# Reordering the last twelve tiles of the prologue of an attention and feed-forward kernel: four tiles of v last, a flag one tile sooner, statistics in one place

## Time and profile before

| | us |
|---|---|
| median of 3 runs | 3751.72 (3751.03 to 3753.09) |
| the profiled execution's own time | 3749.25 |
| its span | 3747.5 |
| TensorE busy | 3704.4 (99%) |
| VectorE, ScalarE, GpSimd busy | 3153.3, 2795.3, 622.9 |

### The profile page before, as it was taken

How to read it: one execution, slowest core, us unless ns; L and a number is a source line. 1 busy time by engine, 2 the same in 40 slices (tenths; PEclk the granted TensorE clock), 3 DMA queues, 4 the chain that set the end, 5 groups by cost and what they waited for, 6 DMA issues and landing times.

```text
span 3747.5 us, 57714 instructions
## 1 busy us (share of the span) xinstructions
PE 3704.4 (99%) x21736; PEld 2051.2 (55%) x21736; DVE 3153.3 (84%) x2918; ACT 2795.3 (75%) x3626; POOL 622.9 (17%) x281
## 2 busy tenths in 40 slices
PE   7999999999999999999999999999999999999999
PEld 6344444444444444444444444444468888888887
DVE  6899999999999999999999999988875555555554
ACT  4788888888888888888888888889873333333333
POOL 0101001023434343223222301320020000000000
PEclk9999999999999999999999999999999999999999
DMA  7544444445444544554555444544340101010010
GB/s 246 125 104 101 105 105 105 106 99 110 101 101 101 111 106 96 112 113 104 113 110 117 98 99 103 120 100 115 78 152 23 45 23 45 23 45 23 29 40 23
DMA packets 255351, 344.58 MB, mean 92 GB/s; under 512 B 118000, under 2 KB 142576, under 8 KB 254000
## 3 DMA queue, kind: packets, MB, share of 16 engines
q1 hardware_dynamic: 251504, 324.43, 36.8%
q0 software_dynamic: 3392, 15.73, 1.4%
q10 hardware_dynamic: 128, 0.03, 0.0%
HBM read 198.55 MB, written 131.07 MB: 88 GB/s over the span
## 4 chain that ended last, share of the span: by engine, by line
PE 89%; DVE 7%; issue 2%; ACT 1%; DMA 0%; DVEq 0%; ACTq 0%; SPq 0%
PE ps L887 22%; PE ps L862 16%; PE ps L956 13%; PE ps L1014 12%; PE ps L800 9%; DVE acc L1652 5%; PE ps L942 5%; PE ps L803 4%; PE ps L910 3%; PE ps L961 2%; PE ps L772 1%; PE ps L1050 1%; ACT pr L1282 1%; PE ps L923 1%; PE ps L1035 1%
## 5 line engine op out<-in xcount | busy, mean ns | idle before, releaser
L1282 ACT ACTIVATE pr<-ps 128x1024 f32<-128x1024 f32 x2048 | 1990.4, 1029 | 257.6 <-PE ps L862 251.0
L1652 DVE TENSOR_TENSOR acc<-acc,pr 128x2048 f32<-128x2048 f32 x768 | 1780.7, 2319 | 41.1 <-ACT pr L1282 11.7
L887 PE MATMUL ps<-pr,vst 128*32 128x512 f32 x8192 | 1011.2, 600 | 0.0
L862 PE MATMUL ps<-qst,kst 50*128 50x512 f32 x4096 | 781.9, 456 | 9.9 <-ACT pr L1282 7.5
L862 PEld LDWEIGHTS ps<-qst,kst 50*128 50x128 f32 x4096 | 337.2, 184 | 658.8 <-ACT pr L1282 463.7
L887 PEld LDWEIGHTS ps<-pr,vst 128*32 128x32 f32 x8192 | 213.3, 109 | 446.6 <-issue 433.5
L1451 ACT ACTIVATE rb<-ps,scf 128x512 f32<-128x512 f32 x228 | 157.0, 689 | 350.5 <-PE ps L961 350.5
L1014 PE MATMUL ps<-tP,hh_ 128*128 128x512 f32 x1024 | 399.6, 390 | 1.4 <-DVE hl_ L1873 1.4
L1014 PE MATMUL ps<-tP,hl_ 128*128 128x512 f32 x1024 | 398.8, 389 | 0.0
L800 PE MATMUL ps<-xt,wqh 128*128 128x512 f32 x1024 | 376.8, 419 | 3.0 <-DVE xt L1542 3.0
L478 POOL TENSOR_SCALAR xin<-xin,mv,rs 128x512 f32<-128x512 f32 x60 | 205.7, 3432 | 876.5 <-DVE rs L1571 876.5
(11 more groups left out here) (179 smaller groups left out, 3822.8 us busy)
## 6 DMA issues: line engine op xcount, KB each, us to landing
qst<-q_scratch SPq DMA_DIRECT2D x128, 256.0 KB, 4.7
kst<-k_scratch SPq DMA_DIRECT2D x128, 256.0 KB, 7.1
q_scratch<-stg SPq DMA_DIRECT2D x112, 256.0 KB
k_scratch<-stg SPq DMA_DIRECT2D x112, 256.0 KB
qst<-q_scratch SPq DMA_DIRECT2D x128, 128.0 KB, 5.0
kst<-k_scratch SPq DMA_DIRECT2D x128, 128.0 KB, 7.8
vst<-v_scratch SPq DMA_DIRECT2D x128, 128.0 KB, 4.7
xr<-in_L_attn_x_dram SPq DMA_DIRECT2D x64, 256.0 KB
```

The costliest lines, as they stand in the source:

```text
L862: ins = e.matmul(ps[:, 2 * c + hh, :], kst[rows, r, j, t * 128:(t + 1) * 128], qst[rows, r, j, c * 512:(c + 1) * 512], start=True, stop=True)
L887: ins = e.matmul(ps[32 * c4:32 * c4 + 32, 4 + j, :], vst[:, r, t, 32 * hh:32 * hh + 32], pr[:, sl, c, hh, :], start=(t == 0), stop=(t == 7 ...
L1282: e.activation(pr[:, sl, c, :, :], ps[:, 2 * c:2 * c + 2, :], ACT.Exp, scale=SCALE).then_inc(s_exp, 1)
L1652: e.tensor_tensor(acc[:, j, :], old, new, ALU.add).then_inc(s_add, 1)
```

## The change

The second chunk's order becomes the eight tiles of q and k and then the four of v: T = 12 to 19 are Q8 to Q15, T = 20 to 23 are V4 to V7. Everything of the flag moves one T: TensorE's part and ScalarE's transfers from 21 to 20, VectorE's first part from 20 to 19 and its second from 21 to 20, where it stands behind the last turn of the third chunk. The third chunk's statistics and gathering all run at T = 14 and its refining and normalizing at T = 15; before they ran at T = 14 (three statistics), 15 (the fourth, gathering) and 16 (refining, normalizing). The first and second chunk's statistics stay where they were.

```diff
-         (0, 1, 8, 2, 3, 4, 5, 6, 7, 9, 10, 11))
+         (0, 1, 2, 3, 4, 5, 6, 7, 8, 9, 10, 11))
...
-                if T == 21:
+                if T == 20:
                     pe_tile(e, T, T % 4, 0, 10)
                     pe_flag(e, 0)
                     pe_tile(e, T, T % 4, 10, 12)
...
-                if T == 21:
+                if T == 20:
 
                     sync_shift(e, 0)
...
-                for n in ((0, 1, 2), (3, 4), range(6, 11))[k + 3] if -3 <= k < 0 else ():
+                steps = ((range(5), range(6, 11), ()) if C else ((0, 1, 2), (3, 4), range(6, 11)))
+                for n in steps[k + 3] if -3 <= k < 0 else ():
                     dve_ln_step(e, C + 1, n)
                 if T - 1 in UNIT_AT:
                     dve_ternary(e, UNIT_AT.index(T - 1))
-                if T == 20:
+                if T == 19:
                     dve_flag(e, 0, 0)
                 if 0 <= k < 4:
                     dve_turn(e, C + 1, k, 4 + k)
-                if T == 21:
+                if T == 20:
                     dve_flag(e, 0, 1)
                     flag = load_flag(e, 0)
                     dve_shift(e, flag, 0)
```

## The result

The changed kernel takes 3759.64 us (median of 13 runs, 3754.28 to 3763.01), the kernel before in the same series 3751.31 (13 runs, 3748.08 to 3754.71): 8.3 us more, ratio 1.0021, 95% interval 1.0014 to 1.0028. The forecast was 3759.2. The profiled execution took 3759.76, with a span of 3758.0 against 3747.5 before, so the two traces stand 10.5 apart where the medians stand 8.3 apart; the profiled execution of before was one of its faster ones, by 2 us.

What follows compares the result with a forecast made beforehand. TensorE, busy 99% of the span, bounds the kernel. First score +7.9 and clock -0.4 sum to +7.5: profiled 3749.25 becomes 3756.8, against the median 3759.2 us; range 3753.2 to 3761.5.

Steps and rivals of the forecast that it cites:

- V6's copy waits for V4's store: ScalarE before the first score: V6's copy waits for V4's store to land at 105.7, first score 108.7, +7.9.
- SyncE reaches V4 at 95.2: SyncE's queue: V4's store, behind Q10 to Q15, is issued at 96.53 - 1.28 = 95.2; bound below 93.9.
- Landing 10.5 after the issue, by V5's row: V4's store takes V5's 10.5 from issue to landing, behind Q15: 95.2 + 10.5 = 105.7.
- The low bound from V0's 5.4: Earliest landing of V4's store, with V0's time, little ahead of it: 93.9 + 5.4 = 99.3.
- V6 to V7, 2.89: ScalarE behind V6's copy: `woh` and V7's copy take 2.89 more, and the first score waits for V7.
- The clock, -0.4: TensorE after the longer stall: first scores slow (+0.3), up to 1.3 could come back before the first sum; middle -0.4.
- The turn sooner by 1.85, the flag sooner: Prologue: third chunk's first turn 1.85 sooner, flag one tile sooner; these alone would bring the first score 2.6 sooner.
- The first load of q: SyncE's first q and k loads: issued about 1.3 later, landing near 94.3, covered by the first score at 108.7.
- After the first score nothing follows that depends on the clock of the prologue: First pair: the first score's gain or loss carries to the end in full; sums run at VectorE's own pace.
- rival (b): V4's store: no backlog reaches it, issued by 89, so the flag chain decides: -2.6, 3749.1; chance 0.05.
- The Trainium skill's ring order: Transfer engines: descriptors go in ring order, done only when all engines are, so V4 cannot pass Q15's backlog.
- The Trainium skill's fit of 2.0 us plus size over 436 GB/s: V4's store: 2.6 us estimated for 256 KB, landing 97.8, first score 100.8, no loss; no v store was that short.

Runs made afterwards that it cites:

- 1: Changed kernel with V6 staged in an area of its own, so its copy waits for no store: 3749.89 against 3750.29 for the kernel before.
- 3: Changed kernel with the third chunk's statistics back where they were, only order and flag changed: 3757.50 against 3750.29 for the kernel before.
- 5: Changed kernel with V4's store ahead of Q14's and Q15's in SyncE's queue: 3753.27 against 3750.62 for the kernel before.
- 2: Kernel before with only the third chunk's statistics and normalizing moved as in the change: 3750.04 against 3750.29 for the kernel before.
- 7: Kernel 1 with the staging slots of Q8 to Q15 in the order of their stores: 3750.74 against 3750.62 for the kernel before.
- 9: Kernel 7 with VectorE's second part of the flag ahead of the last turn's low part: 3751.03 against 3750.62 for the kernel before.
- 6: Changed kernel with rounded parts of Q14 and Q15 stored twice, ahead of V4's store: 3763.01 (5 runs) against 3750.03 for the kernel before.
- 4: Changed kernel with V4's store issued by ScalarE on its own queue: 3753.05 against 3750.29 for the kernel before.
- 8: Kernel before with the third chunk's statistics moved and staging slots reordered, measured twice: 3748.83 against 3750.62, then 3751.63 against 3750.03.

## Why the prediction was right

It was right in direction, size and mechanism; some terms were off, and one assumption fell. That the number came within 0.5 us is luck. In the traces the first score is 10.3 later and the span 10.5 longer, where I had 7.9 and 7.5: SyncE's queue and the clock together were some 3 us worse than forecast. The medians lie only 8.3 apart, because the execution of before that I counted from was 2 us faster than its median and the changed kernel's stands at its own.

- **V6's copy waits for V4's store: right.** Taking that wait away takes the loss away (1).
- **SyncE reaches V4 at 95.2: too early, 97.64.** The later start of VectorE has no part in it: at 70.7 the two queues stood at the same place. I had everything to Q15 come sooner by V4's 1.28. Without V4 the queue took from 70.72 to 97.6, 26.9 us, where with V4 it had taken 25.8; in 3 it took 26.5. Taking a v store out of the queue did not shorten it in these traces. Why was not tested, and the queue's pace differs by execution: from Q10's to the end of Q13's store it took 20.5 in the changed kernel and 17.2 in 5, with the same transfers.
- **Landing 10.5 after the issue, by V5's row: right**, 10.4 in the changed kernel, 10.5 in 3. The low bound from V0's 5.4 did not come near: 8.7, with two stores fewer ahead and a queue that had stood still for 4 us (5), is the shortest seen.
- **V6 to V7, 2.89: right**, 108.12 to 111.00.
- **The clock, -0.4: wrong sign.** From the first score to the first sum it took 7.4 (118.53) instead of 7.1. The four slow matmuls cost their 0.5 and nothing came back: the granted clock was still 0.50 from 112 to 116 and 0.56 from 116 to 120.
- **The turn sooner by 1.85, the flag sooner:** 1.45 against the shifted start, and `mh` was issued at 93.33 where I had 91.6: 0.97 is the shift, 0.40 the turn, 0.44 the slow matmuls behind it. The first load of q was issued 3.7 later (81.66 against 77.93), not 1.3. All were hidden behind V6's wait, as forecast, and what was won there had no worth (3).
- **"After the first score nothing follows that depends on the clock of the prologue": wrong.** It holds for a loss. For a gain the exponentials meet stores that have not landed, and VectorE and TensorE meet x and v (1, 2, 7, 9). So the rival (b), -2.6, would by 1 have been nearer 0 even with its landing. The step that I left out is `act_exp`'s wait on the stores whose slots it overwrites: I had named no work that hides it.
- **The Trainium skill's ring order** ("DMA: Bandwidth & Descriptors", "Queues, rings and completion order") agrees: with work taken away ahead of it V4 lands sooner, with more ahead later (5, 6). The same section of the Trainium skill says that an engine takes turns between the queues it has work for. By that V4 on ScalarE's queue shares with SyncE's instead of passing it, which fits the 13.1 of 4, though no view here shows the turns. The Trainium skill's fit of 2.0 us plus size over 436 GB/s ("Anatomy of one DMA" on the same page), which is for transfers that GpSimd issues, gives an estimate of 2.6 us for 256 KB, a quarter of the 10.4 measured here behind a backlog.

## What to carry to other kernels

When a producer is moved later, look not only at who needs its result but at who needs its buffer again: with two areas by parity, four tiles in a row leave two tiles' time for a store, and here a store needed 10 us behind a backlog. The time from issue to landing depends on the backlog at that place, so take it from a transfer that stood at the same place, not from one with little ahead of it. And before counting on an earlier start, list every wait of the next stage on a transfer: those just met show nothing in the trace of before.

## What was not expected of the hardware

The two queues do not make a transfer quick: from the queue that had nothing in it, the same 256 KB took 13.1 us, against 10.4 at the end of the full one (4 and the changed kernel).

TensorE's clock dips in some of the traces and not in others, at the same place of the first pair. There TensorE has four short gaps on exponentials, of 0.3 to 0.9 us; then 16 matmuls take 3.33 us in the changed kernel and 1.92 in kernel 3. The stretches (the last three numbers are granted clock, transfer share, GB/s) of the changed kernel:

```profile
150.00:154.00 4.00, 2.60 (x20) 0.81 (x12) 3.90 (x4) 3.44 (x5) 2.96 (x2) 0.96 0.00 0
154.00:158.00 4.00, 4.00 (x22) 0.89 (x20) 3.90 (x2) 1.34 (x2) 0.00 (x0) 0.61 0.95 198
```

and of kernel 3:

```profile
150.00:154.00 4.00, 2.61 (x24) 1.04 (x24) 3.90 (x4) 3.49 (x4) 2.01 (x1) 1.00 0.12 41
154.00:158.00 4.00, 4.00 (x30) 1.91 (x26) 3.90 (x3) 2.54 (x4) 0.00 (x0) 1.00 1.09 178
```

The gaps before it are the same, 2.60 and 2.61 busy of 4. The granted clock is 0.61 in one and 1.00 in the other (2.4 GHz). Before, the changed kernel, 1, 2 and 7 have the dip; 3, 4, 5, 6 and both traces of 8 do not; 9 has one of the same size elsewhere, soon after its wait for v. It is worth 1.1 to 1.7 us of the "score to sum" column. What decides it was not tested. Whether it is part of why runs of one kernel lie some microseconds apart isn't shown either: the one kernel with two traces has it in neither.
